# Two sets of transposes of quantised rows move from TensorE and ScalarE to DMA transposes issued from SyncE, in a one-core vision-transformer block

## The reference

```python
h = tok(x, W_lin, b_lin)                      # patches @ W_lin.T + b, 198 rows of 192 per image
h = h + attn(layernorm(h))                    # 12 heads of 16, rotary tables, softmax, projection
h = h + ffn(layernorm(h))

def bitlinear(x, w, g):                       # twice in ffn: 192 -> 1024, then 512 -> 192
    x_norm = rmsnorm(x, g)
    x_q = round(x_norm * 127/max|x_norm|) / (127/max|x_norm|)   # per row, integers -128..127
    w_q = clip(round(w / mean|w|), -1, 1) * mean|w|             # ternary weights
    return x_q @ w_q.T
ffn: up, gate = split(bitlinear(x, w_in, g_in)); bitlinear(silu(gate) * up, w_out, g_out)
```

## Time and profile before

| | |
|---|---|
| median of 3 runs | 1251.02 us (1241.33 to 1255.65) |
| the profiled execution | 1250.52 us, its span 1248.7 us, mean granted clock 0.979 |
| TensorE busy | 1185.9 us, 95% of the span |
| VectorE, ScalarE, GpSimd busy | 959.7, 871.2, 891.6 us |
| transposes of xi and yi on TensorE | 198 and 396 |
| copies of xiT and yiT on ScalarE | 37.6 us and 57.8 us busy |
| DMA engines | queue q1 39.1% of 16 engines' span |

### The profile page before, as it was taken

One profiled execution on the slowest core, in us unless ns is written; L12 is line 12 of the kernel. 1 busy time (PEld: TensorE's weight loads), 2 busy tenths in 40 slices (PEclk: granted clock), 3 DMA queues, 4 the chain that ended last, 5 costly groups with the idle time before them and its releaser, 6 DMA issues.

```text
span 1248.7 us, 36954 instructions
## 1 busy us (share of the span) xinstructions
PE 1185.9 (95%) x12229; PEld 847.2 (68%) x12229; DVE 959.7 (77%) x2335; ACT 871.2 (70%) x1736; POOL 891.6 (71%) x1605
## 2 busy tenths in 40 slices
PE   7689999999899999999999999999999999999887
PEld 6466766767676677677667766776767677766566
DVE  3455777788688888788788888887788778888786
ACT  1145667677577777777877777777677677777686
POOL 3755676777577787777887777877677678777354
PEclk9889999999899999999999999999899899999999
DMA  7534432544344443444444444344344434432110
GB/s 195 137 88 115 111 96 71 124 116 103 87 108 125 122 102 96 115 127 100 114 107 123 106 102 107 101 125 107 104 111 99 109 95 119 105 78 66 45 48 30
DMA packets 203948, 129.19 MB, mean 103 GB/s; under 512 B 57449, under 2 KB 203060, under 8 KB 203668
## 3 DMA queue, kind: packets, MB, share of 16 engines
q1 hardware_dynamic: 201188, 123.71, 39.1%
q10 hardware_dynamic: 2576, 3.14, 0.9%
HBM read 66.57 MB, written 10.70 MB: 62 GB/s over the span
## 4 chain that ended last, share of the span: by engine, by line
PE 76%; DMA 7%; DVE 5%; SPq 5%; issue 3%; ACT 3%; POOL 2%; ACTq 0%; POOLq 0%; DVEq 0%
PE turn L537 14%; PE score L595 12%; PE turn L617 10%; PE turn L555 9%; PE turn L646 6%; PE score L575 5%; PE turn L604 4%; DMA qkT<-nmaxT 4%; PE turn L625 3%; DVE nmax L937 3%; PE turn L626 2%; PE turn L563 2%; PE turn L664 2%; PE turn L547 2%; PE turn L519 1%
## 5 line engine op out<-in xcount | busy, mean ns | idle before, releaser
L937 DVE TENSOR_REDUCE nmax<-score 99x8 f32<-99x1584 f32 x192 | 347.3, 1809 | 167.5 <-PE score L575 167.2
L746 ACT ACTIVATE prob<-score 99x1584 f32<-99x1584 f32 x192 | 286.6, 1493 | 105.5 <-PE score L595 104.9
L537 PE MATMUL turn<-wlin,xp 128*128 128x192 f32 x1188 | 231.9, 348 | 7.8 <-DMA xp<-in_x 7.8
L537 PEld LDWEIGHTS turn<-wlin,xp 128*128 128x128 f32 x1188 | 203.1, 200 | 18.0 <-issue 8.9
L595 PE MATMUL score<-qkT 32*99 32x198 f32 x3072 | 181.3, 351 | 20.9 <-DMA qkT<-nmaxT 13.2
L617 PE MATMUL turn<-prob,vaug 99*32 99x198 f32 x3072 | 169.5, 340 | 0.0
L1122 POOL TENSOR_TENSOR yg<-early,gout 128x512 f32<-128x512 f32 x99 | 125.9, 1272 | 56.0 <-ACT yr L810 50.7
L595 PEld LDWEIGHTS score<-qkT 32*99 32x99 f32 x3072 | 117.2, 162 | 64.5 <-issue 38.8
L555 PE MATMUL turn<-wqkv,xT 96*128 96x384 f32 x396 | 151.6, 505 | 0.0
L769 ACT ACTIVATE xiT<-turn 96x256 bf16<-96x256 bf16 x99 | 37.6, 380 | 131.8 <-PE turn L635 131.6
L617 PEld LDWEIGHTS turn<-prob,vaug 99*32 99x32 f32 x3072 | 81.2, 110 | 64.3 <-issue 37.5
(11 more groups left out here) (94 smaller groups left out, 2408.6 us busy)
## 6 DMA issues: line engine op xcount, KB each, us to landing
xp<-in_x SPq DMA_DIRECT2D x63, 588.0 KB, 5.3
qkT<-qkd SPq DMA_DIRECT2D x168, 96.0 KB, 2.3
tab<-joined SPq DMA_DIRECT2D x98, 112.0 KB, 3.0
orec<-rden_kept SPq DMA_DIRECT2D x192, 49.5 KB
out<-h SPq DMA_DIRECT2D x99, 96.0 KB, 3.4
onum<-osb SPq DMA_DIRECT2D x64, 99.0 KB, 2.6
vaug<-vt SPq DMA_DIRECT2D x30, 148.5 KB
onum<-osb SPq DMA_DIRECT2D x64, 49.5 KB, 2.3
```

The costliest lines, as they stand in the source:

```text
L537: last = pe.matmul(turn[:, k, 0:D], xp[:, c, place:place + TILE], wlin[:, c, :], start=(c == 0), stop=(c == KC - 1))
L746: act.activation(prob[:, :, 4 * g:4 * g + 4, :].rearrange("p t r n -> p r t n"), score[0:TT, :, 0:2 * TOKENS].rearrange("p r (t n) -> p r ...
L937: dve.tensor_reduce(nmax[:, b % 2, :, 4 * g:4 * g + 4].rearrange("p t r -> p r t"), score[0:TT, :, 0:2 * TOKENS].rearrange("p r (t n) -> p ...
```

## The change

`transpose_xr`, `transpose_yr`, `copy_xiT` and `copy_yiT` are gone from TensorE and ScalarE. In their place SyncE issues one DMA transpose per tile for `xi` and one for `yi`, SBUF to SBUF. The rows `xi` are padded from 2 x 96 to 2 x 128 columns, with zeros set once by VectorE. `keep_busy` begins once the exponentials are done (step 107) rather than at step 100. Nothing else is moved.

```diff
-LATE = 1
-        xi = sb("xi", [128, 2, D], BF16)
-        xiT = sb("xiT", [DC, TBUF, 2, TILE], BF16)
+        xi = sb("xi", [128, 2, 2 * TILE], BF16)
+        xiT = sb("xiT", [128, TBUF, 2, TILE], BF16)
...
+            def turn_y(i):
+                sp.wait_ge(yi_ready, i + 1)
+                if i >= 2:
+                    sp.wait_ge(ffout_ready, i - 1)
+                sp.dma_start_transpose(yiT[:, i % 2, :, :], yi[:, i % 2, :]).then_inc(yiT_turned[i % 2], 16)
+
+            def turn_x(i):
+                sp.wait_ge(xi_ready, i + 1)
+                if i == 0:
+                    sp.wait_ge(margin_set, 1)
+                if i >= TBUF:
+                    sp.wait_ge(ffin_ready, i - TBUF + 1)
+                sp.dma_start_transpose(xiT[:, i % TBUF, :, :], xi[:, i % 2, :]).then_inc(xiT_turned[i % 2], 16)
...
             for s in range(-1, STEPS):
+                for i in at(PROJ_AT, s - 6):
+                    turn_y(i)
                 for b in at(OUT_AT, 2 * s + 5):
                     place_o(b)
...
                 for b in at(OUT_AT, 2 * s + 4):
                     keep_rden(b)
+                for i in at(PROJ_AT, s - 1):
+                    turn_x(i)
                 for i in tile_at(s + 1):
                     prepare(i)
...
             def ffn_in(i):
...
-                pe.wait_ge(xiT_copied, i + 1)
+                pe.wait_ge(xiT_turned[i % 2], 16 * (i // 2 + 1))
...
-                        last = pe.matmul(turn[:, k + half, :], xiT[:, i % TBUF, c, :],
+                        last = pe.matmul(turn[:, k + half, :], xiT[0:DC, i % TBUF, c, :],
...
             def ffn_out(i):
...
-                pe.wait_ge(yiT_copied, i + 1)
+                pe.wait_ge(yiT_turned[i % 2], 16 * (i // 2 + 1))
...
-                if s >= TILES + LATE:
+                if 2 * s > EXP_AT[-1]:
                     keep_busy(s)
-                for i in at(PROJ_AT, s - 1):
-                    transpose_xr(i)
-                for i in at(PROJ_AT, s - 5):
-                    transpose_yr(i)
...
             def even_x(i):
...
-                    act.wait_ge(xiT_ready, i - 1)
-                act.activation(xi[:, i % 2, :], xr[:, :], ACT.Copy, bias=-MAGIC).then_inc(xi_ready, 1)
+                    act.wait_ge(xiT_turned[i % 2], 16 * (i // 2))
+                act.activation(xi[:, i % 2, :].rearrange("p (c n) -> p c n", c=2)[:, :, 0:DC], xr[:, :].rearrange("p (c n) -> p c n", c=2),
+                               ACT.Copy, bias=-MAGIC).then_inc(xi_ready, 1)
...
             def even_y(i):
...
-                    act.wait_ge(yiT_ready, i - 1)
+                    act.wait_ge(yiT_turned[i % 2], 16 * (i // 2))
...
-                for i in at(PROJ_AT, s - 1):
-                    copy_xiT(i)
-                for i in at(PROJ_AT, s - 5):
-                    copy_yiT(i)
...
+            dve.memset(xi[:, :, :].rearrange("p b (c n) -> p (b c) n", c=2)[:, :, DC:TILE], 0.0).then_inc(margin_set, 1)
```

More of the change, by code:

```diff
@@ L317, in build @@
         ident_ready = sem("ident_ready")
-        xiT_ready = sem("xiT_ready")
-        xiT_copied = sem("xiT_copied")
+        xiT_turned = [sem(f"xiT_turned{p}") for p in range(2)]
+        margin_set = sem("margin_set")
         ffin_ready = sem("ffin_ready")
@@ L329, in build @@
         yr_ready = sem("yr_ready")
-        yiT_ready = sem("yiT_ready")
-        yiT_copied = sem("yiT_copied")
+        yiT_turned = [sem(f"yiT_turned{p}") for p in range(2)]
         ffout_ready = sem("ffout_ready")
@@ L627, in project_out @@
                     .then_inc(proj_ready, 1)
[L629 to L637, removed]
             def ffn_in(i):
@@ L763, in copy_o @@
                 act.activation(osb[:, b % 2, g, :], turn[:, bank_of["pv", n], 0:TOKENS], ACT.Copy).then_inc(o_copied, 1)
[L765 to L770, removed]
             def tanh_gate(i):
@@ L811, in round_y @@
                                bias=MAGIC).then_inc(yr_ready, 1)
[L813 to L817, removed]
-                               ACT.Copy).then_inc(yiT_copied, 1)
             act.dma_start(wlin[:, 0:KC // 2, :], wlin_d[:, 0:KC // 2, :]).then_inc(begun_embed, 16)
```

## The result

The changed kernel takes 1492.6 us (median of 4 runs, 1479.1 to 1502.2) against 1250.6 us for the kernel before on the same chip: ratio 1.191, 95% interval 1.180 to 1.202. The forecast was 1327 us, range 1240 to 1460. The direction and the place (a wait of `ffn_in` for the x transpose) were right; the size was out by 166 us.

A forecast was written before the change was run, and what follows sets the result against it. TensorE, busy 95% of the span with a chain of matmuls from end to end, was taken as the bound. The terms -27 - 4 + 35 + 47 + 26 = +77 us on 1250.5 gave about 1327 us, range 1240 to 1460.

The forecast's parts named there:

- Taken from TensorE: Transposes leave TensorE's chain: 0.33 us a step in 82 steps, 27 us gained.
- The 36 steps: Steps with 2.1 to 2.5 us of room ahead of `ffn_in`: TensorE waits 0.96 us each, +35 us.
- The 17 steps: Steps with less room at `ffn_in` because SyncE was behind: a wait of 2.75 us each, +47 us.
- rival C: Gains and waits at `ffn_in` cancel with an x transpose of 2.5 us: 1270 us; chance 0.18.
- The y transpose: Issued by SyncE at a step's head, needed over 11 us later: a DMA of 5 us is still covered.
- the image and key transfers behind: Behind the transposes in SyncE's queue, issued up to 1.3 us later, but TensorE is later too: counted as nothing.
- The clock: TensorE's clock falls after long stops, 3 us a stop, charged for half of the 17: +26 us.
- The unread matmuls: Those of steps 100 to 106 leave TensorE, three steps counted: -4 us, bounded at +10 if they held up the clock.
- Rival B: Transposes take 4.9 us and SyncE's queue becomes the bound: 1530 us; chance of over 1400 us 0.14.

The follow-up runs named there:

- y_only: Changed kernel with x rows transposed on TensorE and copied by ScalarE again, only y by DMA from SyncE: 1343.1 us (1.081).
- spare_turns: Kernel before plus two unread DMA transposes of constants a tile, issued from SyncE at the change's places: 1406.1 us (1.127).
- spare_plain: Kernel before plus four unread plain DMAs of 8 KB a tile in SyncE's queue at the change's places: 1379.2 us (1.104).
- x_early: Changed kernel with the x transpose issued right after the placing of the values, ahead of row maxima and kept reciprocals: 1452.0 us (1.163).
- x_front: Changed kernel with the x transpose further forward in SyncE's order, ahead of the qkT and vaug placements: 1540.2 us (1.234).
- both_from_act: Changed kernel with both transposes issued from ScalarE behind the copy that makes yi, and three buffers of yiT: 1306.7 us (1.046).
- before_max_act: Kernel before with the four DMAs an image that place the row maxima issued from ScalarE: 1271.6 us (1.016).

## Why the prediction was wrong

By its own steps:

- **Taken from TensorE, 27 us.** Right, where TensorE is not stopped. An undisturbed step took 11.2 us, and the chain lost its transposes.
- **The 36 steps, +35 us.** Right in size, between the same tiles (166.9 to 1108.9 us before, 169.0 to 1303.7 after): 32 waits of 0.3 to 2.5 us, mean 1.07, 34 us.
- **The 17 steps, +47 us: the step that failed.** In the same stretch 22 tiles wait 2.5 us or more, mean 4.8: 105 us. I took "0.65 us of SyncE's time" from the row of a plain DMA; measured are 1.21 and 1.23 us. The two make 2.44 us instead of 1.3. The other half is the landing, 4.5 us in the mean of these tiles where I had put 3.0 for all. Of the 59 us too few, five stops more than counted are 24, and 17 stops of 4.8 us instead of 2.75 are 35. I also read the DMA rows wrongly: they begin with the issuing and hold it, as 2.29 us at 212.43, where the second DMA of line 402 starts. So the nearest row was 2.3 us in all, not 2.9, and in the same way the bounds were 1.4 and 4.55 us, not 1.7 and 4.9. That my 3.0 is near the 2.9 us of the tiles with short waits is luck.
- **The formula of the 17 steps.** In it the transpose's own time cancels: 3.0 comes in with a plus, and 3.0 - 2.04 as the wait before with a minus. It gives 2.75 us for any transpose that takes over 2.04 us, also for rival C, which by it has 47 and not 33 us there, 1283 us in all. So it could not show that a late landing lengthens these stops.
- **The y transpose, and "the image and key transfers behind", nothing.** Wrong. `y_only` gains on TensorE and still loses 96 us; its scores wait 39 us for `qkT<-nmaxT`. The cover named for them did not hold. Rows that show SyncE without a stop for 20 us stood in the prediction, but it never summed the queue over a step: 8.7 of 11.5 us, plus 2.4, leaves 0.4 for all its waits.
- **The clock, +26 us.** The mechanism was right and the size wrong: the remaining matmuls took about 126 us more. Where it was lost can be estimated from the trace, by TensorE's busy time times what was missing of the granted clock. That is 24 us in the kernel before and 160 in the changed one: 88 after the 22 long stops, 4.0 each where I took 3 for half of 17; 30 after the 32 short ones, where I took none; 35 from `ffn_in` of tile 84 to the end and 7 ahead of tile 0; and none after the 27 tiles between that hardly waited.
- **The unread matmuls, -4 us.** The other sign: +6 us (interval 0 to 12); the bound was +10.

Sum as measured over the whole span: -42 of work removed, +152 of stops, +126 of slower matmuls, 236 us, against -31 + 82 + 26 forecast. Rival B (over 1400 us, chance 0.14) has the time, and its turning point was passed: "issuing takes well over 1 us". But its price was built on a landing of 4.9 us in every step, which did not occur, and its sign fits the changed kernel badly: SyncE waits 73.5 us there for the reciprocals alone, and no score waits for `qkT<-nmaxT`, as they do in `spare_turns` (65.8 us) and `y_only` (39.1 us). The issuing price by itself is not enough for B's time either (`spare_plain`, 1379 us).

What is shown: in the kernel before, 2.4 us of issuing a tile on SyncE costs 128 us, with nobody waiting (`spare_plain`); transposes instead of small plain DMAs add some 31 (`spare_turns`); the wait for x in an in-order queue is paid at all three places tried (late, `x_early`, `x_front`); issued from ScalarE the whole change costs 57 us (`both_from_act`). What stays open: how the last 83 us from `spare_turns` to the changed kernel, plus the 42 us of work removed that they hide, divide between queue, landing and clock; why relief of the queue at the late place gave nothing back; and what makes some transposes land after 5 to 7 us. For y the trace names one companion: of the 59 y transposes with an image load (`xp<-in_x`) issued in the 6 us before them 39 took over 3.5 us to land, of the other 40 only 5. For x no such pattern was found. In the stop at 817 us the DMA engines moved little for 2 us, though no less than in the microseconds ahead of it (20 GB/s at 815, 32 at 816) (last columns: granted clock, DMA share, GB/s):

```profile
820.00:821.00 1.00, 0.00 (x0) 0.00 (x0) 0.00 (x0) 0.00 (x0) 1.00 (x2) 0.50 2.45 32
821.00:822.00 1.00, 0.00 (x0) 0.00 (x0) 0.00 (x0) 0.00 (x0) 1.00 (x2) 0.50 0.08 21
```

A share above 1.5 in a microsecond, packets that begin there and last beyond it, occurs 7 times between 400 and 880 us in the changed kernel, 8 in `spare_turns`, 9 in `both_from_act`, and never in the kernel before, in `spare_plain` or in `before_max_act`. Single packets say the same over whole runs: packets of at most 512 B that took over 1 us number 186 in the changed kernel, from 60 to 438 in every kernel with DMA transposes, and none in any of the six without. Both go with the transposes; how, no run tells.

## What to carry to other kernels

Before a DMA is added to a queue, sum the queue's issuing over one step of the critical engine and add the new issuing: near the step's length the second 1.2 us cost three times what the first did here. Then ask what the new DMA waits for: in an in-order queue that wait is handed to everything behind it. The engine that makes the data can be the better issuer: for the transposes ScalarE was, but the maxima, which it makes as well, cost 20 us when they were moved there alone. And price issuing by the DMA's own kind, bounded from both sides, as much as its landing.

## What the runs showed of the hardware

- A DMA transpose of bf16 rows held SyncE for 1.16 us (128x128), 1.21 us (256 columns) and 1.23 us (512 columns), medians of `spare_turns` and the changed kernel: nearly the same for four times the data. On ScalarE the medians were 1.14 to 1.36 us. A plain DMA of 8 KB held SyncE for 0.60 us.
- The transposes brought 82,368 packets and 19.5 MB more on the queue than the earlier trace rows's kernel had, all in packets under 512 B, and raised the queue's share of the DMA engines from 39.1% of a span of 1249 us to 43.0% of 1485 us. From ScalarE, beside the old queue, x transposes landed after 3.6 us in the median instead of 2.4, and y transposes after 4.1 instead of 3.2.
- TensorE's granted clock in the 8 us after `ffn_in` started was 0.58 in the mean after the 22 stops of 2.5 us or more, 0.90 after the 32 shorter ones and 1.00 after the 27 tiles that waited under 0.3 us.
- Loads moved unchanged to a second queue made the kernel before 35 us slower, with SyncE less busy. Why was not followed up.
